# Block normalisations moved from VectorE to ScalarE, as a scale and a shift

## What is computed

```python
def _ln(x):
    m = x.mean(-1, keepdims=True); v = jnp.mean((x - m) ** 2, axis=-1, keepdims=True)
    return (x - m) * jax.lax.rsqrt(v + EPS)

# first layer
h = _ln(x) * (1 + sc_msa) + sh_msa
h = _self_attn(h, w_qkv, b_qkv, w_so, b_so)          # windows of 128, shifted by 64
x = x + h * g_msa
h = _ln(x) * (1 + sc_mca) + sh_mca
h = _topk_cross_attn(h, context, ...)                # top 16 of 64 keys
x = x + h * g_mca
h = _ln(x) * (1 + sc_mlp) + sh_mlp
h = _swiglu(h, w_m1, b_m1, w_m2, b_m2)               # 256 -> 2 x 1024 -> 256
x = x + h * g_mlp
# second layer: cross attention to the same context, without top-k
xq, xkv = _ada_ln(x, ...), _ada_ln(context, ...)
x = x + (softmax(q @ k.T / 4) @ v) @ Wp + bp
```

## Time and profile before

| | |
|---|---|
| median of 3 runs | 1036.91 us |
| the profiled execution | 1035.79 us |
| its span, first to last instruction | 1033.6 us |
| TensorE matmul busy | 897.5 us, 87% |
| VectorE busy | 750.6 us, 73% |
| ScalarE busy | 475.0 us, 46% |
| GpSimd busy | 219.1 us, 21% |
| mean granted TensorE clock | 0.96 of full |
| share of the chain that ended last | TensorE 58%, VectorE 30%, ScalarE 6%, issue 5% |

### The profile page before, as it was taken

One profiled execution on the slowest core, in us unless ns is written; L12 is line 12 of the kernel. 1 busy time (PEld: TensorE's weight loads), 2 busy tenths in 40 slices (PEclk: granted clock), 3 DMA queues, 4 the chain that ended last, 5 costly groups with the idle time before them and its releaser, 6 DMA issues.

```text
span 1033.6 us, 22090 instructions
## 1 busy us (share of the span) xinstructions
PE 897.5 (87%) x8088; PEld 653.4 (63%) x8088; DVE 750.6 (73%) x3953; ACT 475.0 (46%) x792; POOL 219.1 (21%) x162
## 2 busy tenths in 40 slices
PE   6977656998999989998999899998999898767975
PEld 4744543786567756875678656775678566644763
DVE  3647866897579957997589757996599758875322
ACT  3336333625564356526463557426562554315313
POOL 1025411402041404211140404120230303120010
PEclk9988777999999999999999999999999998888999
DMA  8250010000100102000100111000100110000000
GB/s 326 98 168 11 2 42 1 17 2 3 41 17 1 53 18 62 11 2 2 57 2 1 53 50 35 7 2 1 57 2 11 43 31 1 2 1 1 21 1 21
DMA packets 29051, 32.96 MB, mean 32 GB/s; under 512 B 4320, under 2 KB 26000, under 8 KB 28688
## 3 DMA queue, kind: packets, MB, share of 16 engines
q1 hardware_dynamic: 28944, 31.55, 9.4%
HBM read 25.19 MB, written 6.36 MB: 31 GB/s over the span
## 4 chain that ended last, share of the span: by engine, by line
PE 58%; DVE 30%; ACT 6%; issue 5%; DMA 1%; POOL 1%; SPq 0%; DVEq 0%; ACTq 0%; POOLq 0%
PE bank L1314 52%; DVE left L1062 8%; DVE top L1060 6%; DVE negm L1025 3%; DVE arena L1079 3%; PE bank L1481 3%; DVE negm L1087 2%; PE bank L1332 2%; ACT arena L816 2%; DVE arena L1054 1%; DVE xh L973 1%; DVE h_low L1072 1%; ACT hT L705 1%; DVE vpad L1016 1%; DMA w_m<-in_w_ada 1%
## 5 line engine op out<-in xcount | busy, mean ns | idle before, releaser
L1314 PE MATMUL bank<-w_m,arena 128*128 128x256 f32 x512 | 115.2, 387 | 6.1 <-issue 6.1
L601 POOL TENSOR_SCALAR veps<-mv 128x4 f32<-128x4 f32 (+1 forms) x33 | 8.1, 245 | 499.8 <-DVE mv L968 499.7
L1314 PEld LDWEIGHTS bank<-w_m,arena 128*128 128x128 f32 x512 | 98.8, 194 | 20.9 <-issue 6.9
L630 POOL TENSOR_TENSOR eS<-arena,top 128x1024 f32<-128x1024 f32 x32 | 61.9, 1935 | 206.8 <-DVE top L1060 206.7
L1062 DVE MATCH_REPLACE8 left<-top,arena 128x64 f32<-128x64 f32 x512 | 99.8, 208 | 0.0
L1062 DVE MATCH_REPLACE8 left<-top,left 128x64 f32<-128x64 f32 x512 | 99.8, 207 | 0.0
L759 ACT ACTIVATE arena<-bank 128x512 f32<-128x512 f32 x128 | 66.1, 603 | 55.3 <-PE bank L1314 55.3
L805 ACT ACTIVATE rden<-bank,chan 128x512 f32<-128x512 f32 x64 | 44.0, 688 | 102.7 <-PE bank L1314 76.8
L1314 PE MATMUL bank<-qr,w_m 128*128 128x512 f32 x256 | 82.3, 402 | 3.9 <-ACT qr L715 3.2
L1314 PE MATMUL bank<-qr,m_low 128*128 128x512 f32 x256 | 80.4, 396 | 0.0
L1025 DVE TENSOR_REDUCE negm<-bank 128x4 f32<-128x512 f32 x128 | 78.6, 680 | 2.0 <-PE bank L1314 1.9
(11 more groups left out here) (133 smaller groups left out, 1840.7 us busy)
## 6 DMA issues: line engine op xcount, KB each, us to landing
w_m<-in_w_m SPq DMA_DIRECT2D x4, 1024.0 KB, 5.5
xin<-in_x SPq DMA_DIRECT2D x4, 512.0 KB, 3.9
arena<-in_w_m SPq DMA_DIRECT2D x1, 2048.0 KB, 12.4
out<-x SPq DMA_DIRECT2D x4, 512.0 KB, 2.9
arena<-in_w_ada SPq DMA_DIRECT2D x1, 1536.0 KB, 10.8
gate<-gate_rows SPq DMA_DIRECT2D x12, 128.0 KB, 3.6
gated_bias<-gate_rows SPq DMA_DIRECT2D x12, 128.0 KB, 3.8
xin<-in_x SPq DMA_DIRECT2D x4, 384.0 KB, 3.1
```

The source lines that it names most:

```text
L630: nc.gpsimd.tensor_tensor(eS[:], S[:, t, :].rearrange("p (h n) -> p h n", h=H), top[:, :, 0:1].to_broadcast([P, H, LC]), ALU.subtract).the ...
L1314: return nc.tensor.matmul(dst, lhsT, rhs, start=start, stop=stop)
```

## The change

For layers 1 to 4 of each block the normalised tiles are written by ScalarE in place of VectorE: `xh = Identity(rstd * x + shift)`, with `shift = -mean * rstd`. VectorE takes minus mean behind the moments (one operation of 128x4 a layer and block, with a wait in front of it), GpSimd multiplies it by `rstd` after its power (one operation of 128x4, with a wait in front). The semaphore that said "rstd is there" is now raised by that multiply. VectorE's calls of `normalise` go, with their waits for the transposes of the reader before; ScalarE's new `normalise` stands at these places in its queue: layer 2 between `take_probs` and `cross_denominator(2, b)`, layer 1 between `modulated(2, c)` and `query(c)`, layer 3 between `take_scores(c)` and `project_qk(a)`, layer 4 right before `modulated(4, b)`. The normalisation of the context rows (layer 0) stays on VectorE.

```diff
@@ GpSimd, layer_rstd
-                nc.gpsimd.tensor_tensor(rstd[:, layer, 0:tiles], veps[:, layer, 0:tiles], minus_half[:, 0:tiles],
-                                        ALU.pow).then_inc(s_rstd[layer], 1)
+                own.step(nc.gpsimd.tensor_tensor(rstd[:, layer, 0:tiles], veps[:, layer, 0:tiles], minus_half[:, 0:tiles], ALU.pow))
+                own.wait()
+                nc.gpsimd.tensor_tensor(shift[:, layer, 0:tiles], minus_mean[:, layer, 0:tiles], rstd[:, layer, 0:tiles],
+                                        ALU.mult).then_inc(s_rstd[layer], 1)
@@ ScalarE
+            def normalise(layer, n):
+                act.wait_ge(s_rstd[layer], n + 1)
+                src = xin[:] if layer == 1 else x[:, n % BLKS]
+                for t in range(W):
+                    nc.scalar.activation(xh[:, t, :], src[:, t, :], ACT.Identity, bias=shift[:, layer, t:t + 1],
+                                         scale=rstd[:, layer, t:t + 1]).then_inc(s_xh[layer], 1)
...
             def full(a):
                 c, b = a - 1, a - 2
                 take_probs(b)
+                normalise(2, c)
                 cross_denominator(2, b)
                 act.wait_ge(s_cur_middle, 16 * (c // BLKS + 1))
                 modulated(2, c)
+                normalise(1, a)
                 query(c)
                 front_in(a)
                 take_scores(c)
+                normalise(3, b)
                 project_qk(a)
...
                 self_denominator(a, 0)
+                normalise(4, b)
                 modulated(4, b)
@@ VectorE, moments_done
-                i.then_inc(s_mv[layer], 1)
+                own.step(i)
+                own.wait()
+                nc.vector.tensor_scalar(minus_mean[:, layer, 0:tiles], mv[:, layer, 0:tiles, 0], -1.0, 0.0,
+                                        ALU.mult, ALU.add).then_inc(s_mv[layer], 1)
@@ VectorE, full
-                normalise(1, a, (2, c))
-                normalise(3, b, (1, a))
...
-                normalise(4, b, (3, b))
...
-                normalise(2, a, (4, b))
```

More of the change, by code:

```diff
@@ L305, in build @@
         rstd = sb("rstd", [P, 5, W])
+        minus_mean = sb("minus_mean", [P, 5, W])
+        shift = sb("shift", [P, 5, W])
         negm = sb("negm", [P, W, RG, RP])
@@ L832, in first @@
                 exp_tables()
+                normalise(1, 0)
                 act.wait_ge(s_chan, 32)
@@ L859, in second @@
             def second():
+                normalise(2, 0)
                 act.wait_ge(s_cur_middle, 16)
@@ L862, in second @@
                 modulated(2, 0)
+                normalise(1, 1)
                 query(0)
@@ L938, in last @@
                 cross_denominator(4, b)
+                normalise(3, c)
                 modulated_and_rounded(c)
@@ L942, in last @@
                 exp_tables()
+                normalise(4, c)
                 modulated(4, c)
@@ L1165, in first @@
                                         parity[:].unsqueeze(2).to_broadcast([P, 2, KC]), ALU.mult).then_inc(s_q_bias, 1)
-                normalise(1, 0)
                 first_modulations()
@@ L1178, in first @@
                 dve.wait_ge(s_rstd[0], 1)
-                normalise_tiles(0, ctx_rows, ctx_rows, B // 2)
+                for t in range(B // 2):
+                    nc.vector.tensor_scalar(ctx_rows[:, t, :], ctx_rows[:, t, :], mv[:, 0, t, 0:1], rstd[:, 0, t:t + 1],
+                                            ALU.subtract, ALU.mult).then_inc(s_xh[0], 1)
                 early_keys(0)
@@ L1196, in first @@
                 nc.vector.memset(negm3[:].rearrange("p t r n -> p (t r n)"), 0.0)
-                normalise(2, 0, (1, 0))
             def second():
                 first_moments(1)
-                normalise(1, 1, (2, 0))
                 topk(0, 0, (0, 1, 2))
@@ L1222, in second @@
                 topk(0, 3, (0,))
-                normalise(2, 1, (1, 1))
                 topk(0, 3, (1, 2, 3, 4))
@@ L1271, in last @@
                 residual_moments(2, b)
-                normalise(3, b, (2, c))
                 topk(c, 0, (0,))
@@ L1291, in last @@
                 cross_divide(4, b)
-                normalise(3, c, (4, b))
                 residual(4, b, 0)
@@ L1298, in last @@
                 residual_moments(3, c)
-                normalise(4, c, (3, c))
                 last_max(c)
```

## The result

The changed kernel takes 1081.74 us in the median of four runs (1079.99 to 1087.65), beside 1036.66 us for the kernel before. The ratio is 1.0438, with a 95% interval of 1.0393 to 1.0484: slower by 45 us. The profiled execution took 1081.31 us with a span of 1079.4. The forecast was 1080 us, with a range of 1056 to 1098.

What follows compares the result with a forecast made beforehand. Bound: a chain of waits repeated each block, with TensorE or VectorE last. Five blocks 31.8, block a = 2 4.95, ends -0.6 and clock 6.8 made +43 us: forecast 1080 us, range 1056 to 1098.

Steps and rivals of the forecast that it cites:

- Price of a tile: ScalarE's normalisation of four 128x256 tiles: 2.06 us, bounds 1.38 and 2.4, against VectorE's 1.38 us.
- The small steps: Minus mean on VectorE and shift on GpSimd, between moments and tiles: together 0.5 us, bounds 0.35 and 1.5.
- Layer 2: Tiles ahead of the cross denominators in ScalarE's queue make TensorE's projection late: +2.1 us a block, 0.7 in block a = 2.
- Layer 1: Tiles fit into ScalarE's 5.53 us wait for the queries: cost zero.
- Layer 3: After the score copies, GpSimd's delayed additions meet VectorE's h_low: +3.35 us a block, bounds 0.6 and 4.
- The rival without a meeting (1063): h_low does not meet GpSimd's operations: 0.6 instead of 3.35 us in six blocks, 1063 us; chance 0.2, shared with hiding.
- the one in which it is hidden: TensorE's side hides the meeting of h_low and GpSimd: also 1063 us, within the same chance of 0.2.
- Layer 4: In front of window 2, ScalarE's tiles delay hT: +0.9 us a block, bounds 0 and 2; VectorE's saved 1.38 us brings nothing.
- The clock: New gaps make TensorE's granted clock fall: one fall of 1.13 us a block, 6.8 us in all, bounds 0 and 5 a block.
- Ends: Sections outside the steady blocks: -5.1 us (second section, layer 1 of block 1) and +4.5 us (last section), together -0.6.
- Block a = 2: Block before the five steady ones, its rstd long ready: 0.7 + 3.35 + 0.9, so 4.95 us without clock.
- The rival "faster": VectorE limits, so its saved tile time in layers 3 and 4 arrives: 1015 us, or 1026 with half; chance 0.05.

Runs made afterwards that it cites:

- only_layer3: The kernel before with only layer 3's normalisation of all blocks moved to ScalarE; 1059.89 us, ratio 1.0175.
- late_layer2: The kernel before, with VectorE's layer 2 tiles of block 1 in the second section put behind the last top-k; 1032.84 us, ratio 0.9967.
- four single-layer runs: The kernel before with one layer's normalisation on ScalarE: layer 1 1037.22 us, layer 2 1051.51 us, layer 3 1059.89 us, layer 4 1046.1 us.
- held_additions: The kernel before, normalisation still on VectorE, with GpSimd's first addition of a steady block waiting for ScalarE's last score copies; 1062.01 us, ratio 1.0242.
- layer2_two_matmuls: The kernel before with only layer 2 on ScalarE, plus two overwritten matmuls in TensorE's gap ahead of the projection; 1046.4 us, ratio 1.0051.

## Why the prediction was right, point by point

**Price of a tile.** 2.06 us for four was forecast, 2.06 to 2.12 measured. The small steps: 0.5 us, measured 0.20 (minus mean with its wait) and 0.28 (shift with its gap), the same.

**Layer 2**, forecast +2.1 us, measured +1.72 (9.27 to 10.99). Mechanism and place as forecast, the term was mis-sized: I let the two Ln and Exp pairs run 2.6 us. Queued without idle time between the pairs they took 2.38 us (283.09 to 285.47), since the second Ln starts while the first Exp ends. The other 0.2 us: the moments end 0.14 us sooner in the block (3.77 against 3.91), and the first Ln starts before the last tile ends.

**Layer 1**, forecast zero, measured zero.

**Layer 3**, forecast +3.35 us, measured +2.92 in only_layer3 and +2.91 in the changed kernel (36.06 less 31.43 less 1.72). The order of the meeting was as laid out: first h_low behind subtract_max, GpSimd's addition behind it, second h_low behind that; 4.1 us for two. Of the 0.4 us too much, 0.3 lies behind the tiles: the second h_low ends 10.0 us after them, and I had t + 10.3. The rival without a meeting (1063) fell, as did the one in which it is hidden: taking the meeting away gave 2.70 us a block back.

**Layer 4**, forecast +0.9, measured +0.74. VectorE's saved tiles brought nothing, as argued.

**The clock** is the weakest term, and its size was wrong. I took one fall of 1.13 us a block. Without falls the three terms make 112.95 + 1.72 + 2.91 + 0.74 = 118.3; the five blocks average 120.85, so falls, and one late store, cost 2.5 us a block. A fall in the MLP output costs 1.6 us (16.81 against 15.19), where TensorE is last all the way; at the projection the block is about 1.9 us longer (121.82 against 119.96). Each block had the first, two of the five the second, too. The three other terms were some 1 us a block too large, which is why the sum, 7.5 us against 7.7 measured, was so near. The nearness of 1080 to 1081.74 is owed to that, so it is in part luck.

**Ends.** Second section: forecast -5.1 us, measured -5.3 (TensorE's first transposes after the top-k at 158.51 instead of 163.81). Of this, 4.5 is the wait for the last top-k (17.79 to 13.29); the other 0.8 stands in front of it, where late_layer2, with nothing changed up to there, also stands 0.3 earlier than before. Block a = 2: forecast 4.95 and a fall, 6.1 together, measured 117.04 against 111.37, +5.7 with one fall. Last section: forecast 4.5 and a share of the clock term, measured 7.1 us. It begins with the same late projection, and it has 37.6 us at half clock against 30.7 in before. One gain was left out of the forecast: h_low comes later than GpSimd's addition here, so the meeting of the earlier trace rows is gone and the two take 1.36 us instead of 3.53. With it the forecast would have been 2.2 us lower. I did not separate the section further.

**Who waits for whom.** VectorE's h_low and GpSimd's operations never ran side by side at full pace: the first h_low took 1.32 us and the second 2.87, against 0.68 alone. By the Trainium skill ("SBUF — State Buffer", section "Who interferes with whom") a VectorE operation with two SBUF inputs contends with a GpSimd operation that reads SBUF; the trace agrees. The same section says that ScalarE never waits. The moved tiles don't test it: they took 0.58 to 0.66 us each, but those of layer 3 had ended before GpSimd's first addition. What made the price is the order: each of the two h_low had a GpSimd operation ahead of it. The move also takes VectorE's tiles out of such a meeting (one of them took 2.44 us beside a GpSimd addition in before, 0.40 alone), but that came about twice, both times outside the steady blocks (at 77.9 and 857.3 us).

**The rival "faster"** (VectorE is what limits) fell in all four single-layer runs: 24 us less VectorE work, and the only gain, in the second section, comes from a wait for GpSimd and not from the engine.

## What to carry to other kernels

When work is moved to an engine with room, read what its new place in that queue stands in front of, and then who else waits for the moved result: here about half of the loss came through a third engine, GpSimd, whose operations were only shifted, by about 7 us in the block (18.9 to 26.1), into the time of a VectorE operation that waits for them. One line moved took half of the loss away. And price the gaps that a change opens in TensorE twice, once as time and once as clock: two useless matmuls in a gap of 2 us won 5 us by the medians, 10 by the ratios.

## What the runs showed of the hardware

- Two VectorE operations in a row that met a full GpSimd queue alternated with it: each waited for one GpSimd operation, and GpSimd's next was stretched by the VectorE one (2.83 against 2.36, 1.74 against 1.27 us). One meeting cost 2.7 us although both h_low together are 1.28 us long.
- Falls of the clock went with TensorE's longer idle pieces, but not each time. Of the 70 steady blocks of all fourteen traces, 15 have an idle piece of 2.04 to 2.37 us ahead of the projection of layer 2, behind eight transposes of 1.09 us, and 9 of these have a fall that begins there; of the 55 blocks with at most 1.35 us there, or with matmuls in the gap, none has. Ahead of the MLP output 15 blocks have 2.17 us, and 10 have a fall (5 of 5 in the changed kernel, 4 of 5 in held_additions, 1 of 5 in only_layer3); of the 55 with 1.03 to 1.28 us none has. What decides between the blocks with the same gap is open.
- Falls also come about 100 us into a block, in the scores of layer 4, where TensorE's idle pieces are 0.69 and 0.77 us long: one block of five in before, two of five in layer2_two_matmuls.
- What a fall cost depended on where it came: 1.1 us in the block of 114.10 in before, 1.6 us at the MLP output, about 1.9 us at the projection.
